# A selective-scan mixer whose carried-state product is split into 16-bit halves

## The reference, cut to what matters

```python
xdt = xc * dtc[..., None]
scores = einsum('bclhn,bcshn->bchls', Cc, Bc) * Lmat
Ydiag = einsum('bchls,bcshp->bclhp', scores, xdt)
states = einsum('bclhn,bchl,bclhp->bchpn', Bc, decay_states, xdt)
def step(carry, inp):
    st, cd = inp
    new = carry * cd[:, :, None, None] + st
    return (new, carry)
_, prev = jax.lax.scan(step, init, (st_seq, cd_seq))
Yoff = einsum('bclhn,bchpn,bchl->bclhp', Cc, prev, exp(cs))
Y = (Ydiag + Yoff) + x * D
out = rmsnorm(Y * silu(gate), per group) * norm_w @ out_proj_w.T
```

## Time and profile before

| | us |
|---|---|
| median of 3 runs (lowest, highest) | 2434.76 (2432.14, 2435.37) |
| the profiled execution, its own time | 2433.26 |
| its span, first to last instruction | 2431.4 |
| mean granted TensorE clock, share of full speed | 0.987 |
| busy in the span: PE, DVE, ACT, POOL | 2343.2, 1794.1, 1584.3, 1377.3 |

### The profile page before, as it was taken

How to read it: one execution, slowest core, us unless ns; L and a number is a source line. 1 busy time by engine, 2 the same in 40 slices (tenths; PEclk the granted TensorE clock), 3 DMA queues, 4 the chain that set the end, 5 groups by cost and what they waited for, 6 DMA issues and landing times. The chain is left out here.

```text
span 2431.4 us, 49850 instructions
## 1 busy us (share of the span) xinstructions
PE 2343.2 (96%) x16008; PEld 1328.4 (55%) x16008; DVE 1794.1 (74%) x3250; ACT 1584.3 (65%) x3327; POOL 1377.3 (57%) x1178
## 2 busy tenths in 40 slices
PE   6999999999999999999999998879999999999898
PEld 3555555555555555555555554445555556555444
DVE  6777777777777787777777885567787777888613
ACT  6776776776776776776776774355665555655533
POOL 5576576576576576576576579344344434454323
PEclk8999999999999999999999999889999999999999
DMA  7343343343343343343343441320010110100000
GB/s 244 120 134 113 111 136 113 112 137 111 111 137 111 110 136 113 112 137 111 112 137 110 132 152 36 129 89 14 36 40 14 41 36 14 40 10 14 1 1 35
DMA packets 117294, 218.95 MB, mean 90 GB/s; under 512 B 10016, under 2 KB 43424, under 8 KB 115840
## 3 DMA queue, kind: packets, MB, share of 16 engines
q1 hardware_dynamic: 116992, 215.29, 27.0%
HBM read 212.10 MB, written 3.15 MB: 89 GB/s over the span
## 5 line engine op out<-in xcount | busy, mean ns | idle before, releaser
L990 ACT ACTIVATE E<-wq,cst 128x128 f32<-128x128 f32 x1024 | 311.7, 389 | 2.2 <-PEq L298 2.2
L256 DVE SCALAR_TENSOR_TENSOR xc<-bank,taps,xc 128x511 f32<-128x511 f32 (+2 forms) x384 | 283.0, 737 | 24.6 <-ACT xc L243 24.1
L1963 POOL TENSOR_TENSOR qT<-qT,qrot 128x512 f32<-128x512 f32 x64 | 81.3, 1270 | 358.3 <-DVE qrot L1852 358.3
L1297 POOL TENSOR_TENSOR acc<-acc,sq 128x512 f32<-128x512 f32 x112 | 162.6, 1452 | 183.5 <-ACT sq L1002 183.5
L61 PE MATMUL bank<-xhi,wx 128*128 128x512 f16 x640 | 242.7, 379 | 0.0
L60 PE MATMUL bank<-xlo,wx 128*128 128x512 f16 x640 | 242.6, 379 | 0.0
L59 PE MATMUL bank<-xhi,wx 128*128 128x512 f16 x640 | 242.5, 379 | 0.0
L1109 DVE TENSOR_TENSOR E<-E,cbm 128x1024 f32<-128x1024 f32 x128 | 235.0, 1836 | 0.9
L1280 POOL TENSOR_TENSOR ecs<-ecs,xcC 128x768 f32<-128x768 f32 x128 | 235.2, 1837 | 0.4 <-POOLq L298 0.4
L1176 DVE SCALAR_TENSOR_TENSOR u<-xc,D,bank 128x512 f32<-128x512 f32 x128 | 95.7, 747 | 177.1 <-PE bank L815 166.4
L1285 POOL TENSOR_TENSOR xw<-xt,wdec 128x384 f32<-128x384 f32 x128 | 106.5, 832 | 174.5 <-DVE xt L1128 174.4
(11 more groups left out here) (265 smaller groups left out, 6617.3 us busy)
## 6 DMA issues: line engine op xcount, KB each, us to landing
wq<-cs_rows SPq DMA_DIRECT2D x128, 512.0 KB, 4.0
ecs<-ecs_rows SPq DMA_DIRECT2D x128, 384.0 KB, 3.6
wx<-in_w_xbc SPq DMA_DIRECT2D x80, 256.0 KB, 2.6
wz<-in_w_z SPq DMA_DIRECT2D x64, 256.0 KB, 2.6
wo<-in_w_o SPq DMA_DIRECT2D x64, 256.0 KB, 3.9
wq<-in_wq SPq DMA_DIRECT2D x8, 1024.0 KB, 5.6
awo_raw<-in_wo SPq DMA_DIRECT2D x32, 256.0 KB, 3.0
wkv<-in_wkv SPq DMA_DIRECT2D x8, 512.0 KB, 3.7
```

The source lines that it names most:

```text
L256: self.nc.vector.scalar_tensor_tensor(out=dst[:, d:T], in0=self.k.bank[bank][:, 0:T - d], scalar=self.taps[:, bass.ds(g, 1), b, j, 3 - d:4 ...
L990: ins = nc.scalar.activation(E[t.i % 4][:, h, c], sc.csr[t.i % 2][:, h, c * P:(c + 1) * P], ACT.Relu, scale=-1.0, bias=head(sc.cst, t, c, h))
L1297: nc.gpsimd.tensor_tensor(acc[t.b][:], acc[t.b][:], sq[:], ALU.add).then_inc(acc_done, 1)
```

## The change

The carried states and ecs are split into 16-bit halves, and PE forms Yoff as three 16-bit products for each head and chunk in place of one 32-bit product. ACT makes the leading half of the states, DVE their remainder, POOL the remainder of ecs. These three have one buffer each, and st has one in place of two; POOL's split waits for `y_ready` of the tile before. PE's `turn_x` moves ahead of the gate's projection; DVE's `turned_x` moves ahead of all taps of x. On ACT the exponentials move from the start of an even slot to the end of the odd slot ahead of it, so that in ACT's list they stand in the same place. On POOL `decayed_x` moves ahead of the split of `wz`.

```diff
-        st = [sb(f"st{i}", [P, CH - 1, P]) for i in range(2)]
+        st = sb("st", [P, CH - 1, P])
+        sthi, stlo = sb("sthi", [P, CH - 1, P], F16), sb("stlo", [P, CH - 1, P], F16)
+        ecslo = sb("ecslo", [P, 2, T - P], F16)
...
                 def scan(t):
                     pe.wait_ge(m_done, t.n + 1)
-                    pe.wait_ge(cs_done, t.n + 1)
+                    pe.wait_ge(cs_lo, t.n + 1)
+                    pe.wait_ge(st_lo, t.n + 1)
                     pe.wait_ge(gz_done, t.n + 1)
...
-                        for h in range(2 if c else 0):
-                            r = slice(h * HD, (h + 1) * HD)
-                            mm = nc.tensor.matmul(Y[r, cols], st[t.i % 2][:, c - 1, r], sc.ecs[t.i % 4][:, h, (c - 1) * P:c * P],
-                                                  start=False, stop=True, skip_group_check=True)
+                        e, d = sc.ecs[t.i % 4], slice((c - 1) * P, c * P)
+                        for x in range(3 if c else 0):
+                            for h in range(2):
+                                r = slice(h * HD, (h + 1) * HD)
+                                mm = nc.tensor.matmul(Y[r, cols], (sthi, sthi, stlo)[x][:, c - 1, r],
+                                                      (lead(e[:, h, d]), ecslo[:, h, d], lead(e[:, h, d]))[x],
+                                                      start=False, stop=x == 2, skip_group_check=True)
...
+                    if tile_at(g, m + 2):
+                        turn_x(g, m + 2)
                     if tile_at(g, m + 1):
                         gate(tile_at(g, m + 1))
-                    if tile_at(g, m + 2):
-                        turn_x(g, m + 2)
...
+                def leading_states(t):
+                    act.wait_ge(s_step, 3 * t.n + 3)
+                    nc.scalar.copy(sthi[:], st[:]).then_inc(st_hi, 1)
...
                     square(s)
                     leading(s)
+                    if tile_at(g, m + 1):
+                        leading_states(tile_at(g, m + 1))
...
+                def rest_of_states(t):
+                    dve.wait_ge(st_hi, t.n + 1)
+                    nc.vector.tensor_tensor(stlo[:], st[:], sthi[:], ALU.subtract).then_inc(st_lo, 1)
...
                         masked(n1)
+                        rest_of_states(n1)
...
+                    if n2:
+                        turned_x(n2)
                     if n3:
-                        taps("x", sc.xc[n3.i % 4], n3, 2 + n3.i, (remainder, lambda: turned_x(n2)))
+                        taps("x", sc.xc[n3.i % 4], n3, 2 + n3.i, (remainder, None))
...
                     nc.gpsimd.tensor_tensor(e[:], e[:], sc.xcC[t.b][:, P:T].unsqueeze(1).to_broadcast([P, 2, T - P]),
                                             ALU.mult).then_inc(cs_done, 1)
+                    pool.wait_ge(cs_done, t.n + 1)
+                    wait(pool, y_ready, t.n)
+                    nc.gpsimd.tensor_tensor(ecslo[:], e[:], lead(e[:]), ALU.subtract).then_inc(cs_lo, 1)
...
-                        if 9 <= mm:
-                            sc.split_wz(pool, s.g + 1, mm - 9)
+                    if tile_at(g, m + 2):
+                        decayed_x(tile_at(g, m + 2))
+                    if more and 9 <= mm:
+                        sc.split_wz(pool, s.g + 1, mm - 9)
```

More of the change, by code:

```diff
@@ L667, in mixer @@
         cs_done, xw_done, acc_done, rstd_done = S("cs_done"), S("xw_done"), S("acc_done"), S("rstd_done")
+        st_hi, st_lo, cs_lo = S("st_hi"), S("st_lo"), S("cs_lo")
         acc_split, xw_lo, bt_done = S("acc_split"), S("xw_lo"), S("bt_done")
@@ L1019, in first @@
                     gate(tile_at(0, 0))
+                    leading_states(tile_at(0, 0))
                     decays(tile_at(0, 1))
@@ L1024, in slot @@
                     s = tile_at(g, m)
-                    if m % 2 == 0:
+                    if isinstance(s.n, int) and s.n == 0:
                         for d in (1, 2):
-                            if tile_at(g, m + d):
-                                exps(tile_at(g, m + d))
+                            exps(tile_at(g, m + d))
                     square(s)
                     leading(s)
+                    if tile_at(g, m + 1):
+                        leading_states(tile_at(g, m + 1))
                     if m % 16 < XT:
@@ L1056, in slot @@
                         turned_B(nu, k.bank[ring_bank(s.b, USE_BT)])
+                    if m % 2:
+                        for d in (2, 3):
+                            if tile_at(g, m + d):
+                                exps(tile_at(g, m + d))
                     if is_last_unit(s):
@@ L1114, in state @@
                         dve.wait_ge(st_ready, t.n + 1)
-                        nc.vector.tensor_copy(st[t.i % 2][:, 0], W[:, 0:P]).then_inc(s_step, 1)
+                        nc.vector.tensor_copy(st[:, 0], W[:, 0:P]).then_inc(s_step, 1)
                         return
@@ L1120, in state @@
                         mm = nc.vector.scalar_tensor_tensor(
-                            out=st[t.i % 2][:, c, r], in0=st[t.i % 2][:, c - 1, r], scalar=head(sc.cd, t, c, h),
+                            out=st[:, c, r], in0=st[:, c - 1, r], scalar=head(sc.cd, t, c, h),
                             in1=W[:, c * P + h * HD:c * P + (h + 1) * HD], op0=ALU.mult, op1=ALU.add)
                     mm.then_inc(s_step, 1)
+                def rest_of_states(t):
+                    dve.wait_ge(st_hi, t.n + 1)
+                    nc.vector.tensor_tensor(stlo[:], st[:], sthi[:], ALU.subtract).then_inc(st_lo, 1)
                 def turned_x(t):
@@ L1168, in first @@
                     masked(tile_at(0, 0))
+                    rest_of_states(tile_at(0, 0))
                     turned_x(tile_at(0, 1))
@@ L1200, in remainder @@
                                                        in1=yhi[s.i % 2][:], op0=ALU.mult, op1=ALU.subtract).then_inc(lo_done, 1)
+                    if n2:
+                        turned_x(n2)
                     if n3:
-                        taps("x", sc.xc[n3.i % 4], n3, 2 + n3.i, (remainder, lambda: turned_x(n2)))
+                        taps("x", sc.xc[n3.i % 4], n3, 2 + n3.i, (remainder, None))
                     else:
                         remainder()
-                        if n2:
-                            turned_x(n2)
                     if nu and s.i == 2:
@@ L1327, in slot @@
                             sc.split_wx(pool, s.g + 1, mm - 7)
-                        if 9 <= mm:
-                            sc.split_wz(pool, s.g + 1, mm - 9)
+                    if tile_at(g, m + 2):
+                        decayed_x(tile_at(g, m + 2))
+                    if more and 9 <= mm:
+                        sc.split_wz(pool, s.g + 1, mm - 9)
                     if m == 16:
                         sc.split_wz(pool, s.g, XT - 1)
-                    if tile_at(g, m + 2):
-                        decayed_x(tile_at(g, m + 2))
                     if is_last_unit(s):
```

## The result

| | before | after |
|---|---|---|
| median of the runs (lowest, highest), us | 2433.45 (2430.66, 2435.37) | 2492.96 (2491.74, 2494.44) |
| ratio to before, 95% interval | | 1.0244 (1.0232, 1.0257) |
| span of the profiled execution | 2431.4 | 2490.1 |
| busy: PE, DVE, ACT, POOL | 2343.2, 1794.1, 1584.3, 1377.3 | 2351.5, 1974.7, 1627.4, 1593.3 |

The changed kernel is 59.5 us slower (2492.96 less 2433.45). The forecast was 2465, range 2430 to 2505: the sign was right, and the size half of what came.

The account below looks back on a forecast made before the run. PE bounds the mixer's middle, POOL its last slots. -16.7 (products) + 31.5 (turn_x) + 7.2 (returns) + 8.8 (end) + 0.7 (start) = +31.5 on 2433.26: 2465 us, range 2430 to 2505.

Parts of the forecast that it names:

- The 16-bit products, -16.7: On PE, three 16-bit pairs of heads take 0.174 us a chunk against 0.2175, saving 16.7 us over 128 tiles.
- The rival of unpaired heads: On PE, 16-bit pairs keep the 32-bit pace of 0.109, so the products' term is +42: 2524 us; chance 0.06.
- `turn_x`, +31.5: PE's turn_x waits for states made late by POOL's ecs remainder beside the gate's multiplication: 105 slots by 0.30 us, +31.5.
- The loop's return, +7.2: Where the loop goes round, turn_x waits for the states after a late u: 1.20 us more at six returns, +7.2.
- The mixer's end, +8.8: At the mixer's end POOL sets the pace; six remainders of 1.47 us move scan 127 and what follows, +8.8.
- The start, +0.7: Scan 0 waits for DVE's E, behind which the remainder of the states now stands: +0.7 us.
- Costed at nothing, ACT: ACT's copy is covered by 1.76 us of room ahead of the scan, and the exponentials keep their list place: 0.
- Costed at nothing, DVE's remainder of the states: DVE's remainder takes at most 0.68 us, covered by 0.68 idle ahead of u: 0; otherwise u is late by the excess.
- The multiplication comes first: Rival: DVE's gate multiplication goes ahead of POOL's new split, so the 31.5 term is gone: 2433.3 us; chance 0.17.
- POOL and DVE take turns all the time: Rival: their instructions exclude each other, ecs is late in most slots, wait 0.60 to 0.99: 2496 to 2537; chance 0.10.
- the wait of 0.60 a slot: Upper bound taken for PE's wait ahead of turn_x: 63 us in place of 31.5, giving 2496 us.
- Nothing but PE's saving: Rival: the multiplication comes first, POOL's end has room and the returns cost nothing: 2416.6 us; chance 0.09.

Follow-up runs that it names:

- run 7: Kernel before's order with the three 16-bit products, halves stale after the first tile, no split on ACT, DVE or POOL from then on: 2416.60 us.
- run 12: As run 10, but DVE makes the remainder of the states for the first tile alone, stale after; POOL's remainder made for every tile: 2430.85 us.
- run 10: Changed kernel without ACT's copy, POOL's remainder written into ecs itself, PE's turn_x in the middle of the gate's projection; nothing left out: 2461.22 us.
- 6: Changed kernel, POOL's remainder written into the lower halves of ecs itself, without the wait for the scan before: 2490.14 us.
- run 1: Kernel before with only the three moves of order (turn_x, turned_x, decayed_x); Yoff stays one 32-bit product: 2444.42 us.
- run 3: Changed kernel, but POOL makes the remainder of ecs for the first tile alone, stale after; all products stay: 2461.82 us.
- run 5: Changed kernel without ACT's copy: PE and DVE take the upper half of the 32-bit states as leading half; nothing left out: 2491.18 us.
- run 9: Changed kernel with halves in place (no ACT copy), PE and DVE in the order of before, DVE's remainder of the states directly behind E: 2520.07 us.

## Why the prediction was right in sign and short by half

Runs 7, 12, 10, 6 and the changed kernel form a chain: 2416.6, 2430.9, 2461.2, 2490.1, 2493.0. The second differs from the first by POOL's remainder and the places of the moves, then come DVE's remainder (30.4), `turn_x` put ahead of all of the gate's projection, with ACT's copy (28.9), and the buffer and place of `ecslo` (2.8, within the noise of the two medians). The prices depend on the order in which things are taken away: from the changed kernel itself, POOL's remainder brings 31.1 and DVE's 20.0, since each leaves waits that the other also fills.

- **The 16-bit products, -16.7.** Right: run 7 gives -18.1. The rival of unpaired heads falls. So does the figure of the Trainium skill's "TensorE: Matmul & The Clock Gate", section "Back-to-back issue gap", named there: no 81 ns for a product of 128 columns, but 0.06 us for a pair, also on halves of the columns.
- **`turn_x`, +31.5.** The size is right: 0.27 a slot in slots 2 to 15 where 0.30 was taken; by 105 slots that is 28. Run 10 gives 28.9 with the returns in it. POOL's remainder takes the worked-out 1.47, and run 1 shows the room that is lost. The mechanism is right for most of the even slots, where u starts 1.74 to 1.76 after the scan and the gate's multiplication takes 1.15 to 1.82: 2.2 of the 3.85 a group. (In slots 10 and 12 it is ecs under way, not the split, that holds the multiplication up.) In the odd slots, the other 1.65, u itself starts 2.1 to 2.5 after the scan, since DVE's list of the slot before ends late, and in five of the seven the multiplication takes 0.68 to 0.78. That lateness was costed at nothing (below), so the size came out right in part by luck.
- **The loop's return, +7.2.** Under-priced for the order alone: in run 1 slot 1 is 12.65 us long and was 11.06, 1.59 in place of 1.20; by six 9.5, the most of that run's 12.2. In the changed kernel slot 1 takes 11.63, only 0.57 more, and slot 0 ahead of it, which ends with the wait for gz, 1.31 more; what the return costs there by itself the runs don't tell.
- **The mixer's end, +8.8.** Right: 9.6 in the changed kernel, of which run 3, without POOL's remainder, loses 9.1 (84.0 from scan 120 to 127); between scans 112 and 127 run 12 takes 7.7 more than run 7.
- **The start, +0.7.** Not settled: scan 0 starts at 58.85 and started at 57.33, but the traces of the runs have it anywhere from 55.98 to 59.67.
- **Costed at nothing, ACT.** Right for the copy, within noise: run 5. The exponentials keep their place in the list, but they now hand on the lateness of the silu ahead of them.
- **Costed at nothing, DVE's remainder of the states.** This is the step that failed. The prediction held it to be "no longer than the gate's multiplication, 0.68", and set against it 0.68 of idle time ahead of u, read from one slot. It takes 1.15, and the idle time in the kernel before was 0.14 in slot 3, 0.31 in slot 9 and 0.45 in slot 5. The prediction had itself read, a few lines earlier, that a DVE instruction with two SBUF tensors waits for the POOL instruction under way, and its sum had used it for the gate's multiplication alone. It holds for the new remainder too, for ylo, and against the whole of POOL's list. Its own warning, "if that cover goes, u comes late by the excess", is what happened: B's remainder, the taps and the silu came late with u. Its price is 30.4, by runs 10 and 12; that is the work together with what POOL adds to its length, which no run takes apart. The forecast was 28 too low.
- **The rivals.** "The multiplication comes first" fell: in slots 0, 10 and 12 the multiplication does begin behind ecs, ahead of the split, but it takes 1.16 there, 0.48 late, more than the 0.35 of room. "POOL and DVE take turns all the time" (2496 to 2537) had a part of the mechanism: 90 of the 96 multiplications between scans 16 and 112 begin while an instruction of POOL is under way, and began so in 28 before. But it looked for the price ahead of `turn_x`; it came at the gate and at B's remainder. The measured time lies near its lower end and near the forecast's own upper bound (2496), but the wait of 0.60 a slot that both stand for did not come. "Nothing but PE's saving" (2416.6) is the time of run 7, which leaves the splits out.

## What to carry to other kernels

When work is added to an engine that shares a port with another, size it by how long such an instruction takes beside the other's list as it is (here 1.15, where the shortest was 0.54), and set the sum of all lengthened instructions against the idle time of every kind of slot (here 0.14 to 2.67 ahead of u), not against one slot. An engine that is 78% busy in a stretch can have next to no room in some of its slots; look for the chains that its lateness feeds, through other engines' lists, to the one that sets the end. Before splitting an operand to speed up a product, run the product alone on stale halves: that is the most that the split can pay.

## What the runs showed that was not expected

Freeing POOL's remainder from its wait changed nothing: 2490.1 against 2493.0, the gate's multiplication 1082 and 1072 ns. The load on the shared port by itself does not set how long DVE's instructions take, either: in the nine runs in which POOL is busy for 694 to 720 of the 909 us, the changed kernel among them, the gate's multiplication takes 955 (run 10) to 1466 ns (run 9) on average. Where the two lists meet counts too. And on ACT an instruction of 64 columns took 337 ns beside 389 for 128, so that a multiplication cut by head and chunk took 1.5 us a tile where POOL took 0.83.
